# Chunked cross-attention on one core: the output product moved into the round of its own attention

## The reference, cut to what matters

```python
scores = jnp.einsum('bnqhd,bnkhd->bnhqk', qh, kh) * scale
scores = scores + jnp.where(km[:, :, None, None, :] > 0, 0.0, NEG)
attn = jax.nn.softmax(scores, axis=-1)
out = jnp.einsum('bnhqk,bnkhd->bnqhd', attn, vh).reshape(N, T, C)
out = (out @ W_out.T + b_out).transpose(0, 2, 1) * masks
...
out = out + x
mu = jnp.mean(out, axis=2, keepdims=True)
var = jnp.mean(jnp.square(out - mu), axis=2, keepdims=True)
return (out - mu) * jax.lax.rsqrt(var + EPS)
```

## Time and profile before

| | us |
|---|---|
| median of 3 runs | 1950.19 (1943.25 to 1955.95) |
| profiled execution, span | 1939.0 |
| TensorE matmul busy | 1891.7 (98%) |
| VectorE busy | 1703.2 (88%) |
| GpSimd busy | 1504.6 (78%) |
| ScalarE busy | 1330.1 (69%) |

### The profile page before, as it was taken

How to read it: one execution, slowest core, us unless ns; L and a number is a source line. 1 busy time by engine, 2 the same in 40 slices (tenths; PEclk the granted TensorE clock), 3 DMA queues, 4 the chain that set the end, 5 groups by cost and what they waited for, 6 DMA issues and landing times.

```text
span 1939.0 us, 90624 instructions
## 1 busy us (share of the span) xinstructions
PE 1891.7 (98%) x40488; PEld 1608.1 (83%) x40488; DVE 1703.2 (88%) x1577; ACT 1330.1 (69%) x1792; POOL 1504.6 (78%) x1059
## 2 busy tenths in 40 slices
PE   7999999999999999999999999999999999999994
PEld 6888888888888888888888888888888888888882
DVE  4898889899999978998988999888899889989986
ACT  5667667767767766776777677677667767767762
POOL 4677778878888778878777887787778778778874
PEclk9999999999999999999999999999999999999997
DMA  5667778777777767777777777777777777777766
GB/s 171 159 181 215 218 206 224 215 218 223 212 220 222 213 196 217 222 215 215 221 219 212 221 222 214 222 210 215 212 221 219 215 217 216 222 209 222 208 176 195
DMA packets 242882, 409.60 MB, mean 211 GB/s; under 512 B 28992, under 2 KB 94784, under 8 KB 242496
## 3 DMA queue, kind: packets, MB, share of 16 engines
q1 hardware_dynamic: 242496, 403.82, 74.2%
HBM read 168.82 MB, written 67.11 MB: 122 GB/s over the span
## 4 chain that ended last, share of the span: by engine, by line
PE 96%; DVE 1%; issue 1%; ACT 1%; DMA 0%; POOL 0%; SPq 0%; DVEq 0%
PE proj_bank L313 38%; PE proj_bank L370 19%; PE proj_bank L347 19%; PE score_bank L386 11%; PE o_bank L419 9%; DMA b_cols<-b_in 0%; ACT prob L478 0%; ACT score_bank L470 0%; DVE squares L673 0%; SPq L256 0%; POOL prob L557 0%; DVE stats L700 0%; POOL y L575 0%; DMA prob_t<-squares 0%; DVE sums L657 0%
## 5 line engine op out<-in xcount | busy, mean ns | idle before, releaser
L557 POOL TENSOR_TENSOR prob<-prob,recip 128x1024 f32<-128x1024 f32 x256 | 482.0, 1904 | 46.5 <-DVE recip L665 46.5
L575 POOL TENSOR_TENSOR y<-y,x_raw 128x512 f32<-128x512 f32 x256 | 331.5, 1295 | 181.1 <-DVE y L691 181.1
L565 POOL TENSOR_TENSOR ctx_lo<-ctx_raw,ctx_hi 128x512 fp32r<-128x512 f32 x255 | 330.2, 1295 | 171.9 <-ACT ctx_hi L458 159.7
L500 ACT ACTIVATE k_f<-proj_bank,b_cols 128x512 f32<-128x512 f32 x256 | 176.4, 689 | 365.2 <-PE proj_bank L313 365.2
L646 DVE TENSOR_REDUCE row_max<-score_bank 128x32 f32<-128x2048 f32 x128 | 293.4, 2292 | 138.7 <-PE score_bank L386 138.7
L313 PE MATMUL proj_bank<-ctx_hi,w_hi 128*128 128x512 f32 x1024 | 337.1, 410 | 3.0 <-DVE ctx_lo L630 3.0
L313 PE MATMUL proj_bank<-ctx_hi,w_lo 128*128 128x512 f32 x1024 | 322.1, 396 | 0.7 <-issue 0.7
L313 PE MATMUL proj_bank<-ctx_lo,w_hi 128*128 128x512 f32 x1024 | 322.1, 396 | 0.0
L657 DVE TENSOR_REDUCE sums<-prob 128x16 f32<-128x1024 f32 x256 | 309.3, 1209 | 5.0 <-ACT prob L478 5.0
L650 DVE TENSOR_TENSOR prob<-score_bank,row_max 128x2048 f32<-128x2048 f32 x128 | 293.3, 2292 | 4.4
L673 DVE STREAM_TRANSPOSE squares<-prob 128x2048 f32<-128x2048 f32 x128 | 294.6, 2301 | 2.6 <-POOL prob L557 2.6
(11 more groups left out here) (45 smaller groups left out, 3487.1 us busy)
## 6 DMA issues: line engine op xcount, KB each, us to landing
prob_t<-squares SPq DMA_DIRECT2D x1024, 128.0 KB
ctx_raw<-ctx SPq DMA_DIRECT2D x128, 512.0 KB, 4.8
x_raw<-x SPq DMA_DIRECT2D x128, 512.0 KB, 4.8
out<-y SPq DMA_DIRECT2D x128, 512.0 KB, 4.3
mask_all<-mask SPq DMA_DIRECT2D x128, 256.0 KB, 4.2
v_x<-v_f SPq DMA_DIRECT2D x256, 128.0 KB, 3.4
y<-w_in_t SPq DMA_DIRECT2D x1, 768.0 KB, 5.6
y<-w_out_t SPq DMA_DIRECT2D x1, 256.0 KB, 6.7
```

The costliest lines, as they stand in the source:

```text
L557: pool.tensor_tensor(part, part, half(slots(recip[:, n % 2, :]), i), ALU.mult).then_inc(norm_done, 1)
L565: pool.tensor_tensor(ctx_lo[:, n % 2, :, tokens], ctx_raw[:, n % BLOCKS, :, tokens], ctx_hi[:, n % 2, :, tokens].bitcast(F32), ALU.subtrac ...
L575: pool.tensor_tensor(part, part, x_raw[:, m % 2, f, :], ALU.add).then_inc(added, 1)
```

## The change

The output product of block p-1 is made in round p, straight after its product with values, and not a round later. TensorE's order becomes S(p+1), K and Q(p+2), PV(p-1), V(p+2), O(p-1) in both halves. The loop has two passes fewer, of which one was used for work. The waits for banks follow the new order: K waits for y, O waits for the eviction of V, V for that of Q. `context_ready`, `rows_ready` and `probs_ready` are the same waits as before, in the same places ahead of K, S and PV. ScalarE splits the context first in its round and interleaves exponentials with queries and mask rows with values; VectorE takes the statistics one block earlier, o_lo between the two sums, and the outputs last; GpSimd adds x first in its round; SyncE stores one round's output a little differently and issues the eight probability transfers with b as the outer loop. `LEAD` and `PIECE_WAITS` keep their values.

```diff
-            for p in range(-3, ALL + 4):
+            for p in range(-3, ALL + 2):
...
+                wait(sp, pv_done, n)
                 sp.wait_ge(turned, n + 1)
-                wait(sp, pv_done, n)
-                for f in range(HALVES):
-                    for a in range(2):
-                        for b in range(2):
+                for b in range(2):
+                    for f in range(HALVES):
+                        for a in range(2):
...
-                if there(m + 4):
-                    pe.wait_ge(q_f_done, 2 * (m + 4) + f + 1)
-                elif there(m + 3):
+                if there(m + 3):
                     pe.wait_ge(v_f_done, 2 * (m + 3) + f + 1)
...
             def step(p):
                 met(PIECE_WAITS)
+                rows_ready(p + 1)
                 scores(p + 1)
+                context_ready(p + 2)
                 project_k(p + 2, 0)
                 project_k(p + 2, 1)
                 project_q(p + 2, 0)
                 project_q(p + 2, 1)
                 if p == -1:
                     output_bias()
-                project_out(p - 2, 0)
+                probs_ready(p - 1)
                 probs_times_v(p - 1)
-                project_out(p - 2, 1)
                 project_v(p + 2, 0)
                 project_v(p + 2, 1)
+                project_out(p - 1, 0)
+                project_out(p - 1, 1)
...
+                split_ctx(p + 3, 0)
+                split_ctx(p + 3, 1)
                 keys(p + 2, 0)
-                split_ctx(p + 3, 0)
                 keys(p + 2, 1)
-                split_ctx(p + 3, 1)
                 queries(p + 2, 0)
+                exponentials(p + 1, 0)
                 queries(p + 2, 1)
-                exponentials(p + 1, 0)
                 exponentials(p + 1, 1)
-                lay_negatives(p + 2, 0)
-                lay_negatives(p + 2, 1)
                 high_attention(p - 1)
                 values(p + 2, 0)
+                lay_negatives(p + 2, 0)
+                values(p + 2, 1)
+                lay_negatives(p + 2, 1)
...
+                add_residual(p - 2, 0)
+                add_residual(p - 2, 1)
                 low_ctx(p + 3, 0)
                 low_ctx(p + 3, 1)
                 if p >= 0:
                     masked_keys(p + 2)
...
-                add_residual(p - 2, 0)
-                add_residual(p - 2, 1)
                 divide(p + 1, 0)
                 divide(p + 1, 1)
...
                 turn(p)
-                statistics(p - 3)
+                statistics(p - 2)
...
-                output(p - 2, 0)
                 sum_up(p + 1, 0)
-                output(p - 2, 1)
+                low_attention(p - 1)
                 sum_up(p + 1, 1)
                 reciprocals(p + 1)
-                low_attention(p - 1)
+                output(p - 1, 0)
                 if done:
-                    mean_shift((p - 3) // BLOCKS)
+                    mean_shift((p - 2) // BLOCKS)
+                output(p - 1, 1)
```

More of the change, by code:

```diff
@@ L285, in step @@
                 move_probs(p)
-                if p == ALL + 2:
-                    for n in range(p - 7, ALL):
+                store(p - 7)
+                if p == ALL + 1:
+                    for n in range(p - 6, ALL):
                         store(n)
-                elif p < ALL + 2:
-                    store(p - 7)
             periods(step)
@@ L315, in project_qk, with context_ready @@
                 last.then_inc(proj, 1)
+            def context_ready(n):
+                if not there(n):
+                    return
+                pe.wait_ge(ctx_hi_done, 2 * (n + 1))
+                pe.wait_ge(ctx_lo_done, 2 * (n + 1) - 1)
+                if n == 0:
+                    pe.wait_ge(ctx_lo_first, 1)
             def project_k(n, f):
@@ L320, in project_k @@
                     return
[L321 to L326, removed]
+                if there(n - 4):
+                    pe.wait_ge(y_done, 2 * (n - 4) + f + 1)
+                else:
+                    wait(pe, v_f_done, 2 * (n - 1) + f + 1 if n else 0)
                 project_qk(n, f, k_proj, C)
@@ L337, in project_v @@
                     return
[L338 to L341, removed]
+                pe.wait_ge(q_f_done, 2 * n + f + 1)
                 for t in range(2):
@@ L372, in project_out, with rows_ready @@
                 last.then_inc(out_proj, 1)
-            def scores(n):
+            def rows_ready(n):
                 if not there(n):
@@ L380, in scores @@
                 pe.wait_ge(seeded, 2 * (n + 1))
+            def scores(n):
+                if not there(n):
+                    return
                 for c in range(CPB):
@@ L401, in open_banks, with probs_ready @@
                 last.then_inc(opened, 1)
-            def probs_times_v(n):
+            def probs_ready(n):
                 if not there(n):
@@ L412, in probs_times_v @@
                 pe.wait_ge(moved[n % MOVES], 128 * (n // MOVES + 1))
+            def probs_times_v(n):
+                if not there(n):
+                    return
                 for c in range(CPB):
@@ L523, in step @@
             def step(p):
+                split_ctx(p + 3, 0)
+                split_ctx(p + 3, 1)
                 keys(p + 2, 0)
-                split_ctx(p + 3, 0)
                 keys(p + 2, 1)
-                split_ctx(p + 3, 1)
                 queries(p + 2, 0)
+                exponentials(p + 1, 0)
                 queries(p + 2, 1)
-                exponentials(p + 1, 0)
                 exponentials(p + 1, 1)
-                lay_negatives(p + 2, 0)
-                lay_negatives(p + 2, 1)
                 high_attention(p - 1)
                 values(p + 2, 0)
-                if p == ALL + 2:
-                    for n in range(p - 7, ALL):
+                lay_negatives(p + 2, 0)
+                values(p + 2, 1)
+                lay_negatives(p + 2, 1)
+                if p == ALL + 1:
+                    for n in range(p - 6, ALL):
                         normalise(n)
-                elif p < ALL + 2:
-                    normalise(p - 7)
-                values(p + 2, 1)
+                else:
+                    normalise(p - 6)
             periods(step)
@@ L607, in step @@
                     masked_keys(p + 2)
[L608 to L613, removed]
+                if p < ALL + 1:
+                    normalise(p - 6)
+                if there(p - 2) and (p - 2) % BLOCKS == BLOCKS - 1:
+                    reciprocal_std((p - 2) // BLOCKS)
+                if p == ALL + 1:
+                    for n in range(p - 6, ALL):
                         normalise(n)
-                add_residual(p - 2, 0)
-                add_residual(p - 2, 1)
                 divide(p + 1, 0)
@@ L731, in step @@
                 turn(p)
-                statistics(p - 3)
-                done = there(p - 3) and (p - 3) % BLOCKS == BLOCKS - 1
+                statistics(p - 2)
+                done = there(p - 2) and (p - 2) % BLOCKS == BLOCKS - 1
                 if done:
-                    mean_and_variance((p - 3) // BLOCKS)
-                output(p - 2, 0)
+                    mean_and_variance((p - 2) // BLOCKS)
                 sum_up(p + 1, 0)
-                output(p - 2, 1)
+                low_attention(p - 1)
                 sum_up(p + 1, 1)
                 reciprocals(p + 1)
-                low_attention(p - 1)
+                output(p - 1, 0)
                 if done:
-                    mean_shift((p - 3) // BLOCKS)
-                if p == ALL + 2:
+                    mean_shift((p - 2) // BLOCKS)
+                output(p - 1, 1)
+                if p == ALL + 1:
                     normalise_last()
```

## The result

The changed kernel takes 1995.98 us in the median (4 runs, 1994.89 to 1999.47), the kernel before in the same comparison 1948.57: ratio 1.0231, 95% interval 1.0203 to 1.0259. It is 2.3% slower. The profiled execution has a span of 1994.7 us and 1996.47 us in all. So only 1.8 us lie around a span here, and the 11.2 us that the prediction took for this were mostly the spread between runs of the kernel before.

The account below looks back on a forecast made before the run. TensorE's list was taken as the bound: span 1939.0 + 3 (beginning and end) - 8 (old stalls) + 2 (o_lo) + 34 (new stalls) = 1970, plus 11.2 to the median, 1981 us; range 1942 to 2018.

Parts of the forecast that it names:

- What bounds the kernel: TensorE's list of six groups, back to back at 14.66 us a round; nothing that another engine gains counts.
- Where the crossings lie: Borders of 256-instruction pieces in TensorE's list: every second round at S 4, K 4, PV 107, S 68, PV 43.
- The stall's price: TensorE waits for instructions at the 4th K matmul every second round: 34 us in all, bounds 0 and 81.
- What goes: The four old instruction stalls inside PV and the slow matmuls after the longest vanish: 8 us gained.
- Seams: Changes between small and large matmuls on TensorE cost the same as before: 0, with 12 us either way.
- Banks: TensorE's waits for evictions ahead of O and for y ahead of K: all hidden, at least 0.6 us left.
- o_lo: VectorE's o_lo, due for O's fifth matmul, is 0.1 us late every fourth round: 2 us in all.
- Beginning and end: First rounds +5.4 us from ScalarE's evictions, last block -2 to -3: together +3 us, bounds 0 and +6.
- The sum: 1939.0 + 3 - 8 + 2 + 34 = 1970 us of span; with 11.2 us to the median, 1981.
- (A): Rival: no stall at the new crossings, as the list is prefetched; 1947 us, chance 0.34 together with (C).
- (B): Rival: TensorE's clock falls after every fifth new stall, 37 us more, 2018 us; chance 0.10.
- (D): Rival: VectorE becomes the bound, o_lo late by 0.5 us in each round, 2011 us; chance 0.06.

Follow-up runs that it names:

- LEAD 68: The changed kernel with LEAD 68 for 102, TensorE's instruction list 17 instructions earlier: 1939.64 us, ratio 0.9983 to the kernel before.
- mean and variance behind o_lo: The changed kernel with its list 17 instructions earlier, and VectorE's mean and variance moved from ahead of o_lo to behind it: 1936.04 us, ratio 0.9942.
- PIECE_WAITS 0: The changed kernel with PIECE_WAITS 0 for 5, so 637 instructions a round and not 640, and borders that drift: 2021.2 us, ratio 1.0418.
- LEAD 172: The changed kernel with LEAD 172 for 102, TensorE's instruction list 35 instructions later: 2049.51 us, ratio 1.0534 to the kernel before.
- LEAD 172 and the late release: The changed kernel, list 35 instructions later, ScalarE normalising ahead of the mask rows' second half, which releases S 0.8 us later: 2118.09 us, ratio 1.0864.
- LEAD 52: The changed kernel with LEAD 52 for 102, the list 25 instructions earlier, giving S its old place in its piece: 1943.43 us, ratio 0.9991.

## Why the prediction was right, by its steps

**What bounds the kernel** held: every us of the difference is on TensorE's list. **Where the crossings lie** held to the matmul: K 4 in every second round, and no other place.

**The stall's price** was the right mechanism at half its size, and it is the term of the sum that was mis-sized: 34 us expected, 72 measured. Three numbers make the difference. The release was put 1.25 us ahead of S and came 1.15 ahead. From release to going on 3.84 us were taken from one case; the mean of all is 4.38: the packet begins 1.72 us after the release, is under way 1.22, and TensorE goes on 1.38 after it has landed. And the fourth matmul was taken as due 2.35 us after S; but what needs the new piece is at the latest its weight load, due at 1021.47 + 0.23 - 1019.67 = 2.03. So 4.38 - 1.15 - 2.03 = 1.20 a pair of rounds, where 0.3 stood, and 61 of them 73 us. The allowance for late fetches, 16 us, is no term of its own in this: they are in the mean of 4.38. The upper bound of 81 us took 1.3 us a stall where its own working gave 1.4.

**What goes**: 8 us expected, about 9 measured. **Seams**: 0, with 12 us either way, and they gave 11: V and O in one stretch take 3.04 + 2.78 = 5.82, while 1.59 + 2.88 + 1.41 = 5.88 stood before, and the seam in S that alternated before is mostly gone. Which seam it is wasn't tried by itself. **Banks**: no wait for v_f or y in the middle, as worked out. **o_lo**: 2 us; in the changed kernel nothing, as the stall of K covers it, but with the stall gone (LEAD 68) O takes 3.16 and not 2.88 us in every fourth round (medians), which makes some 7 us. The 13 us that the expectation for mean and variance behind o_lo names are idle time of the weight loads and not of the matmuls. **Beginning and end**: +5.4 and -2 to -3 expected, +5.8 and -2.5 measured.

**The sum** was 1970 for the span, and 1994.7 came: +38 for the stall, -11 for the seams, the rest small. From span to median 11.2 us were added, and only about 1.8 are there. So it is in part luck that 1981 lies within 15 us of 1996: the stall alone was off by 38 us, and the seams and the 11.2 us, both wrong the other way, gave back some 20.

**Rivals.** (A), no stall, has fallen. With it falls the reading of the Trainium skill (Runtime: NRT & Kernel Launch, Instruction fetch mechanics) by which TensorE's list has room for 2048 instructions: whatever the room, no second piece was there when two borders lay 2.0 us apart; and a border isn't "mostly hidden" where the next one is near. Its 256 instructions for a block fit the drift of the list with PIECE_WAITS 0. (B), the clock, was put at every fifth stall and came once in the middle, behind a stall of 1.55 us: K and Q then took 6.81 us for 22 matmuls, with a granted clock of 0.50 for 3.4 us. With LEAD 172 and the late release it came 26 times, behind stalls of 1.5 to 2.7 us, while others there of up to 2.4 us had no such fall; what decides it isn't shown. (D): VectorE had its pause in every round.

## What to carry to other kernels

A fully unrolled kernel on TensorE has a second schedule, that of its instruction list. As these runs fit it, the list comes in pieces of 256 instructions, and the next piece is asked for only over 25 instructions into the present one and not past a wait that isn't met. Where two borders are passed close together, as in dense groups of small matmuls, TensorE can stand, and the profile calls it "issue". 2.0 us apart it stood every time, and 4.2 us apart at LEAD 172 too; 3.3 and 4.05 us apart (LEAD 52 and 68) it stood in PV in only 12 of some 60 cases. So the distance alone doesn't decide it: the waits that hold the request count as well. After any reordering, look where the borders now fall, and move the list by a few idle instructions at its start before judging the new order: here this was worth 2.5% (ratio 0.998 with LEAD 68 against 1.023), some 50 us, and the order itself nothing that can be measured.

## What was unexpected

The time from release of a wait to going on behind the next border is nearly fixed where the release comes shortly ahead, 4.38 and 4.41 us in two kernels whose stalls differ by 0.7 us, and 4.2 and 4.1 us in the two with LEAD 172; with a release 2.7 us ahead it was 6.1. The next piece is asked for behind the border and not at it: a wait that stands 25 to 28 instructions behind it still delays it (packet 3.1 us behind the border, 3.8 with the release 0.7 us later). And cutting the probability transfers by 31/32 of their bytes shortened the time from release to going on by 0.4 us. Why the packet asked for in PV comes some 2.8 us behind its border in the new order and 1.5 to 1.8 in the old one stays open; the one try at it failed for another reason.
